# A transformer layer on eight cores: a PSUM copy moved from VectorE to ScalarE, FFN products regrouped, and the quantisation threshold computed one tile earlier

## The reference, cut to what matters

```python
q, k, v = x @ Wq.T + bq, x @ Wk.T + bk, x @ Wv.T + bv      # split in 16 heads
q_kern = exp(q - max(q)); k_kern = exp(k - max(k))          # per head
kv = einsum('bhsd,bhse->bhde', k_kern, v); k_sum = sum(k_kern, axis=2)
denom = einsum('bhqd,bhd->bhq', q_kern, k_sum) + 1e-6
y = einsum('bhqd,bhde->bhqe', q_kern, kv) / denom
x = layernorm(x + y @ Wo.T + bo)
Wt = clip(round(W / (mean(abs(W)) + 1e-5)), -1, 1)          # for W1 and W2
x = layernorm(x + relu(x @ W1t.T + b1) @ W2t.T + b2)        # 4096 hidden columns
```

## Time and profile before

| | us |
|---|---|
| median of 2 runs | 3678.13 |
| the two runs | 3638.76 and 3717.51 |
| the profiled execution | 3642.55 |
| its span, slowest core (3) | 3641.0 |
| spans of the eight cores | 3627.4 to 3641.0 |
| mean granted clock of TensorE, eight cores | 0.974 to 0.975 |
| busy: TensorE (PE) | 3346.2, 92% of the span |
| busy: VectorE (DVE) | 1377.4, 38% |
| busy: ScalarE (ACT) | 910.7, 25% |
| busy: GpSimd (POOL) | 120.9, 3% |

### The profile page before, as it was taken

The page is one execution under the profiler, slowest core; times in us unless marked ns, Lnnn a source line. Parts: engine busy times, 40 slices in busy tenths (PEclk is TensorE's granted clock), DMA queues, the critical chain, the costliest instruction groups (busy, mean ns, idle before and its releaser), DMA issues.

```text
span 3641.0 us, 53913 instructions; the slowest of 8 cores (3627.4 to 3641.0 us)
## 1 busy us (share of the span) xinstructions
PE 3346.2 (92%) x19971; PEld 2010.3 (55%) x19971; DVE 1377.4 (38%) x1935; ACT 910.7 (25%) x1601; POOL 120.9 (3%) x253
## 2 busy tenths in 40 slices
PE   4999889997989898989999999999999999898987
PEld 1445444553656565656565655556565656565655
DVE  4555366654333323242424242323232333323231
ACT  2110000001223232323232232323232323232322
POOL 0000011000000000000000000000000000000000
PEclk9999989998999999999999999999999999999989
DMA  5453155542425252525242434333342424252423
GB/s 179 156 164 118 57 173 162 168 150 71 136 74 158 75 160 74 168 65 171 67 154 79 142 103 126 115 109 125 102 131 90 148 75 157 76 161 72 157 76 130
DMA packets 247423, 443.43 MB, mean 122 GB/s; under 512 B 22640, under 2 KB 88192, under 8 KB 247168
## 3 DMA queue, kind: packets, MB, share of 16 engines
q1 hardware_dynamic: 226688, 370.24, 33.3%
q0 software_dynamic: 20480, 69.75, 5.5%
HBM read 406.34 MB, written 33.56 MB: 121 GB/s over the span
## 4 chain that ended last, share of the span: by engine, by line
PE 83%; DVE 8%; ACT 3%; DMA 3%; issue 2%; DVEq 0%; ACTq 0%; POOL 0%; SPq 0%; POOLq 0%
PE p L947 22%; PE p L996 11%; PE p L1006 10%; PE p L285 4%; PE p L288 4%; PE p L291 4%; PE p L297 4%; PE p L294 4%; PE p L305 4%; PE p L850 3%; PE p L887 2%; PE p L890 2%; PE p L893 2%; PE p L899 2%; PE p L896 2%
## 5 line engine op out<-in xcount | busy, mean ns | idle before, releaser
L996 PE MATMUL p<-x1Th,w1s 128*128 128x256 bf16 x4096 | 923.0, 273 | 26.9 <-DVE x1Tl L754 26.9
L1006 PE MATMUL p<-x1Tl,w1s 128*128 128x256 bf16 x3584 | 811.8, 273 | 0.0
L1017 DVE SCALAR_TENSOR_TENSOR hl<-h,hh 128x256 bf16<-128x256 f32 x512 | 217.6, 425 | 1226.7 <-ACT h L1013 1218.5
L947 PE MATMUL p<-w2s,hh 128*128 128x512 bf16 x2048 | 609.0, 379 | 25.2 <-DVE hl L1017 24.9
L947 PE MATMUL p<-w2s,hl 128*128 128x512 bf16 x2048 | 609.0, 379 | 0.0
L1010 ACT ACTIVATE hh<-p,b_c 128x256 bf16<-128x256 f32 x512 | 242.8, 474 | 1007.1 <-PE p L1001 1001.5
L996 PEld LDWEIGHTS p<-x1Th,w1s 128*128 128x128 bf16 x4096 | 401.1, 98 | 128.5 <-issue 30.4
L1006 PEld LDWEIGHTS p<-x1Tl,w1s 128*128 128x128 bf16 x3584 | 351.0, 98 | 91.9
L947 PEld LDWEIGHTS p<-w2s,hl 128*128 128x128 bf16 x2048 | 200.1, 98 | 241.8
L947 PEld LDWEIGHTS p<-w2s,hh 128*128 128x128 bf16 x2048 | 196.1, 98 | 175.4 <-issue 44.2
L1013 ACT ACTIVATE h<-p,b_c 128x256 f32<-128x256 f32 x512 | 242.7, 474 | 48.8 <-ACT hh L1010 1.9
(11 more groups left out here) (155 smaller groups left out, 4331.2 us busy)
## 6 DMA issues: line engine op xcount, KB each, us to landing
w1s<-w1q SPq DMA_DIRECT2D x467, 256.0 KB, 3.0
w2s<-w2q SPq DMA_DIRECT2D x467, 256.0 KB, 2.6
xg<-xfm SPq DMA_DIRECT2D x64, 512.0 KB, 6.7
wsl<-w1r SPq DMA_DIRECT2D x64, 512.0 KB, 4.5
wsl<-w2r SPq DMA_DIRECT2D x64, 512.0 KB, 4.2
xt<-xtm SPq DMA_DIRECT2D x32, 512.0 KB, 3.6
out<-ot POOLq DMA_DIRECT2D x32, 512.0 KB, 4.3
w1s<-w1q POOLq DMA_DIRECT2D x45, 256.0 KB, 3.1
```

Source lines behind the costliest of these rows:

```text
L947: stf=stf, spf=spf: e.matmul(PB[4 + 2 * ti + nci][:, 0:512], hbuf[:, ti * 128:(ti + 1) * 128], w2s[wb][:, nci * 512:(nci + 1) * 512], star ...
L996: e.matmul(hp[:, 0:TG * 128], w1s[wb][:, fc, :], x1Th[par][:, fc, :], start=(fc == 0), stop=False), waits=w)
L1006: hp=hp: e.matmul(hp[:, 0:TG * 128], w1s[wb][:, fc, :], x1Tl[par][:, fc, :], start=False, stop=False))
L1017: e.scalar_tensor_tensor(hl[cb][:], h32[cb][:], 1.0, hh[cb][:], op0=OP.mult, op1=OP.subtract), waits=((sS, e_h32),))
```

## The change

Four edits are made.

1. `emit_gamma_finalize` is emitted at the end of tile 15 of sequence 0, no longer after tile 0 of sequence 1.
2. The copy of the transposed q out of banks p4 and p5 (L832) is a ScalarE activation with Identity, no longer a VectorE copy. The later users of these banks wait for ScalarE's count (`f4s`, `f5s`), and the y products wait for both engines.
3. `emit_x1tr` also notes when x1Th is ready (`x1T_hi_rr`).
4. In mm1 the eight products with x1Th stand first and the eight with x1Tl behind them. The first set waits for x1Th alone, the second for x1Tl.

```diff
@@ phase 1, end of a tile
             pend_kv = (i, kb, ev_kk, ev_vevac)
+            if si == 0 and i == NT - 1:
+                emit_gamma_finalize()
             if si == 1 and i == 0:
-                emit_gamma_finalize()
                 emit_seq_boundary(0)
@@ emit_x1tr
                     st2["x1T_rr"][par][rr] = e_lo
+                    st2["x1T_hi_rr"][par][rr] = e_hi
@@ emit_attn_rest
-                e_qsT_r[rr] = ev("vector", sV, lambda e, rr=rr, ti=ti,
-                                 bankQ=bankQ: e.tensor_copy(
+                e_qsT_r[rr] = ev("scalar", sS, lambda e, rr=rr, ti=ti,
+                                 bankQ=bankQ: e.activation(
                     qsT[ti][:, rr * 4:(rr + 1) * 4, :].rearrange(
-                        "p a b -> p (a b)"), bankQ[:, 0:512]),
+                        "p a b -> p (a b)"), bankQ[:, 0:512], AF.Identity),
                     waits=((sT, max(e_tr, st2["qsT_free"][ti])),))
-                st2[fv] = e_qsT_r[rr]
+                st2[fs] = e_qsT_r[rr]
...
-                        w = ((sV, max(st2[fv], e_qsT_r[rr])),
-                             (sG, e_kvz[si]))
+                        w = ((sV, st2[fv]), (sG, e_kvz[si]),
+                             (sS, e_qsT_r[rr]))
@@ emit_ffn
                     w = (e_w1,
-                         (sV, max(st2["h_evac"][cb], st2["x1T_rr"][par][0],
+                         (sV, max(st2["h_evac"][cb],
                                   st2["qb_evac"][0] if c < 2 else 0)),
-                         (sS, st2["h_hi"][cb]))
+                         (sS, max(st2["h_hi"][cb],
+                                  st2["x1T_hi_rr"][par][0])))
                 elif fc == 4:
-                    w = ((sV, st2["x1T_rr"][par][1]),)
+                    w = ((sS, st2["x1T_hi_rr"][par][1]),)
                 silent("tensor", lambda e, c=c, fc=fc, wb=wb, par=par, hp=hp:
                        e.matmul(hp[:, 0:TG * 128], w1s[wb][:, fc, :],
                                 x1Th[par][:, fc, :],
                                 start=(fc == 0), stop=False), waits=w)
+            for fc in range(NP):
+                w = ()
+                if fc == 0:
+                    w = ((sV, st2["x1T_rr"][par][0]),)
+                elif fc == 4:
+                    w = ((sV, st2["x1T_rr"][par][1]),)
```

More of the change, by code:

```diff
@@ L577, in build_program @@
         "x1T_rr": [[0, 0], [0, 0]],
+        "x1T_hi_rr": [[0, 0], [0, 0]],
         "x1_ready": [0, 0, 0, 0],
@@ L1002, in emit_ffn @@
                         hp[:, 0:TG * 128], w1s[wb][:, fc, :],
-                        x1Tl[par][:, fc, :], start=False, stop=True))
+                        x1Tl[par][:, fc, :], start=False, stop=True), waits=w)
                 else:
@@ L1007, in emit_ffn @@
                         hp[:, 0:TG * 128], w1s[wb][:, fc, :],
-                        x1Tl[par][:, fc, :], start=False, stop=False))
+                        x1Tl[par][:, fc, :], start=False, stop=False),
+                        waits=w)
             st2["w1_free"][wb] = e_mm1
```

## The result

The changed kernel takes 3533.1 us (median), the kernel before 3642.7 us. The ratio is 0.971 with a 95% interval of 0.968 to 0.974, so it is faster by 2.9%. The forecast was 3536.7 us.

The account below looks back on a forecast made before the run. TensorE carries 83% of the chain of waits, so its idle time or slow clock is what can be gained. 3642.55 - 86.4 - 6 - 3.5 + 8 - 8 + 0 - 10.0 gives 3536.7 us; range 3512 to 3585.

Parts of the forecast that it names:

- The middle groups: FFN end to output projection: with q's copy on ScalarE the projection starts 6.17 us earlier, 14 groups, 86.4 us.
- The first and the last group: Same stage in the end groups: projection earlier by 6 us in the first, 3.5 us in the last.
- nearest case: Last group before the change: idle 1.88, transposes 1.06, idle 1.32 us, and the clock fell while TensorE waited.
- The clock: Y products and tile 1's transposes: half clock still in 3 groups, some 2.6 us each, 8 us given back.
- Rival 1: Y-product stage: the clock still falls in nearly every group, giving 3565 us; chance 0.12.
- mm1: First FFN matmuls: hi products wait only for x1Th, most of the 1.73 us wait moves; 0.5 us by 16 groups, 8 us.
- The new weight blocks: mm1's new order: 8 more new weight blocks a chunk, 512 chunks, at most 18 us, taken as 0.
- rival 3: All mm1 matmuls: a new weight block in every step is not hidden, up to 447 us, 3984 us; chance 0.03.
- Gamma: Quantisation threshold computed one tile earlier: L451 runs at about 448.1 instead of 458.12, 10.0 us gained.
- Rival 2: Y-product stage: ScalarE becomes the late engine, only the visible wait is gained, 3570 us or some 3585; chance 0.10.

Follow-up runs that it names:

- the filling: Changed kernel plus unread TensorE products, 4 ahead of the q transposes and 2 between them and the y products: 3531.4 us, ratio 0.969.
- the changed kernel with the late split: Changed kernel with load and split of the next x tiles emitted behind the y products: 3530.9 us, ratio 0.970 against the kernel before.
- the copy alone: Kernel before with only the copy of the transposed q moved to ScalarE: 3556.1 us, ratio 0.975.
- the late split alone: Kernel before, copy of q left on VectorE, load and split of the next x tiles emitted behind the y products: 3597.4 us, ratio 0.985.

## Why the prediction was right

**The middle groups, 6.17 us each.** Measured 6.05 in the profile. Over all 14, with the groups in which the clock fell, the way from the last pair to the projection took 220.7 us before and takes 138.2 now: 82.5 us, where 86.4 less 8 were forecast. Every start of the replay was met within 0.15 us: copy behind transposes 0.78 (0.75 in the replay), y products behind transposes 1.69 (1.60), tile 1's y products 5.30 (5.19), projection 7.16 (7.05). The releasers were the ones named: the banks for tile 0 (L1045), ScalarE's queue for tile 1.

**The first and the last group, 6 and 3.5 us.** From the first transposes to the projection the first group now takes 856.59 - 842.24 = 14.35 us against 867.83 - 847.59 = 20.24, so 5.9 us. In the last group it is 3367.72 - 3360.55 = 7.17 against 10.56, so 3.4 us on these two cores. The row that the prediction took for its nearest case was an exception, though. On the other seven cores of the same execution of the kernel before, the last group's products ran at full clock behind the same gaps, here on core 0:

```profile
3452.32 1.07 PE L822 MATMUL p<-ident,qs 128*128 128x128 f32 x8 [1.88 <-DVE ot L1034]
3454.70 2.02 PE L850 MATMUL p<-qb,kv 128*128 128x128 f32 x16 [1.32 <-DVE qb L832]
```

There the last group gains 1.7 us only, and the sign that the clock falls with no gap above 1.88 us was one core in eight.

**The clock, 8 us given back in 3 groups.** This term was sized too large for the changed kernel, and it is the only one clearly off. Half clock still occurred in the first group, which the 5.9 us already contain, and in two middle groups near the start. In the chain of waits in order of time (start, duration, piece) their y products read:

```profile
1018.42 3.48 PE p L853 x16
1023.47 2.02 PE p L853 x16
1187.33 2.04 PE p L853 x16
...
1355.02 2.82 PE p L853 x16
1359.40 2.02 PE p L853 x16
```

From tile 0's to tile 1's products it is 5.05 and 4.38 us there, against 3.61 in a group at full clock, so 1.4 and 0.8 us: 2.2 us in all, not 8. The term was too large in both factors: two groups and not three, and less than 2.6 us for each, since only a part of a set was slow (3.48 and 2.82 us, where a whole slow set takes 3.75). The other cores agree: five of the eight have the same two groups, three have none, 10 of 112 middle groups in all. That is also why the filling found nothing to gain in the changed kernel.

How often the clock falls does not follow from the gaps alone, and what decides it is not shown. With the same gaps of 1.88 and 0.63 us it is 13 of 112 middle groups in the changed kernel with the late split and 29 of 112 with the copy alone, where the slowest core lost 6 us in four groups. So that the loss was only 2.2 us is in part luck: in such a neighbour the 8 us would have been near.

Rival 1 (the clock falls in nearly every group, 3565 us) is out. Its mechanism is real, though: it held back the kernel with the late split alone, where 84 of 112 groups were slow. The shorter second gap, 0.63 us against 1.32 there, goes with far fewer falls.

The Trainium skill ("TensorE: Matmul & The Clock Gate", section "HAM oscillation") would have no group slow with gaps under 1.9 us. The changed kernel is nearer to that than my 8 us were. But the traces do not agree with it: in all three kernels with these gaps some groups fell, 10, 13 and 29 of 112.

**mm1, 8 us.** In 13 of the 14 groups of the profile that show it the sixteenth product starts 3.89 us behind the x1 transposes (once 4.24) and started 4.40 behind them before. 0.5 by 16 is 8 us; the run of this edit alone gave 11, with 7 to 20 in its interval. That most of a wait of 1.7 us is moved and not gained was the right reading, and reading the 26.9 us as the gain would have been wrong by a factor of over two by the median. The new weight blocks cost nothing that can be seen (term 0, bound 18 us): the steps stayed at 0.109 us, and rival 3 falls with that.

**Gamma, 10 us.** 9.5 us in the profile, 10.5 us in the run alone. The x load that is now queued behind the two reads cost no more than foreseen: VectorE's split starts at 433.5 on the scale of the earlier trace rows and ends at 434.8 (436.7 was expected), and K's evacuation follows it.

**The sum.** 14 x 6.05 + 5.9 + 3.4 - 2.2 + 8 + 9.5 = 109.3 us; the medians differ by 109.6 us; the forecast was 105.9. The clock's term alone would have made the gain 5.8 us larger than forecast; the middle groups' 6.05 for 6.17 takes 1.7 of that back and gamma 0.5. The mechanisms were the ones named, and only the clock's price was clearly off. Rival 2 (ScalarE is the late engine and only the wait goes, 3570 us) named the right engine for tile 1, with 0.7 us a group, but not its price, since the clock came back.

## What to carry to other kernels

When an engine waits for a short copy, read what stands ahead of the copy in its queue and not how fast the copy is: here the engine's speed is worth 0.1 us a copy, and getting it out of the queue 6 us a group, the clock's 1.7 us on the y products and its share in the next tile included. Replay the stage with the spacings of its own rows, every bank and every queue included, before booking a visible wait as a gain; one wait of 1.7 us gave 0.5, another of 4.0 gave 6, for the clock and the next tile came with it. And look at TensorE's granted clock behind every gap of a microsecond or more.

## What the runs showed of the hardware that was not expected

TensorE's clock fell to half with no idle gap above 1.9 us. With gaps of 1.88 and 1.32 us and 1.06 us of work between them, the products behind them were slow in 84 of 112 middle groups of the late split alone; with 1.88 and 0.63 us in 10 of 112 of the changed kernel, but in 29 of 112 with the copy alone. The first of these patterns left the clock full in the last group of the kernel before on seven of eight cores. One core and one group are therefore a poor sample for the clock: count all cores.

Filling the gaps of the kernel before with 256 products that nobody reads, 63.5 us of them by the profile, made it 27 us faster, since half clock had cost 1.7 us on one set of products in each group and delayed the next.
